# A graph network kernel whose weight products run as fillers: Wg and Wm's parts moved ahead of the third batch, the second bias row moved behind the chunk loop

## The reference

```
A = zeros(1024,1024); A[src,dst] += weight;  deg = sum(A, 1);  dinv = deg > 0 ? deg^-0.5 : 0
h = x
for l in 0, 1:                      # D = diag(dinv)
    h = D A D h
    h = h Wg[l] + bg[l]
    h = leaky_relu(h Wm[l] + bm[l], 0.01)
x = layernorm(x + h)
# second block: edge counts C with self loops, dis = (in-degree)^-0.5
h = relu(C' (x W1) + b1);  h = C' (h W2) + b2       # C' = diag(dis) C^T diag(dis)
x = layernorm(x + h)
```

## Time and profile before

| | |
|---|---|
| median of 3 runs | 334.9 us (334.63 to 335.05) |
| profiled execution | 335.47 us |
| its span | 333.6 us |
| TensorE busy | 314.5 us (94%) |
| VectorE busy | 189.0 us (57%) |
| ScalarE busy | 122.0 us (37%) |
| GpSimd busy | 49.9 us (15%) |

### The profile page before, as it was taken

How to read it: one execution, slowest core, us unless ns; L and a number is a source line. 1 busy time by engine, 2 the same in 40 slices (tenths; PEclk the granted TensorE clock), 3 DMA queues, 4 the chain that set the end, 5 groups by cost and what they waited for, 6 DMA issues and landing times.

```text
span 333.6 us, 4919 instructions
## 1 busy us (share of the span) xinstructions
PE 314.5 (94%) x1977; PEld 259.7 (78%) x1977; DVE 189.0 (57%) x333; ACT 122.0 (37%) x253; POOL 49.9 (15%) x54
## 2 busy tenths in 40 slices
PE   2878999998999999999999999999999999999993
PEld 1767786876788888888888888888888888888882
DVE  6998999714544611165643457675953444225664
ACT  3637889546434401134432013233702444220000
POOL 2100000001005970100000011121680000001111
PEclk9999999999999999999999999999999999999998
DMA  6270000700000000000700000006100000000121
GB/s 211 66 254 2 3 2 0 249 6 2 3 0 1 2 0 0 2 0 0 238 15 0 2 0 0 0 4 226 61 2 0 0 0 2 0 4 33 63 84 73
DMA packets 8590, 13.43 MB, mean 40 GB/s; under 512 B 1906, under 2 KB 2290, under 8 KB 8564
## 3 DMA queue, kind: packets, MB, share of 16 engines
q1 hardware_dynamic: 8564, 13.05, 11.6%
HBM read 10.95 MB, written 2.10 MB: 39 GB/s over the span
## 4 chain that ended last, share of the span: by engine, by line
PE 88%; DVE 7%; issue 2%; ACT 1%; DMA 1%; POOLq 0%; POOL 0%; SPq 0%; ACTq 0%
PE psum L650 75%; PE psum L708 6%; PE psum L636 3%; DVE hot L1004 2%; PE psum L755 1%; DVE sel L996 1%; PE psum L830 1%; DVE hot L999 1%; PE psum L692 1%; DVE wm_low L1089 1%; DVE wgt_low L1076 1%; PE psum L714 1%; DMA src_i<-in_src 1%; PE psum L864 1%; ACT hot L455 0%
## 5 line engine op out<-in xcount | busy, mean ns | idle before, releaser
L441 POOL TENSOR_TENSOR small<-small 128x1 f32<-128x1 f32 x16 | 11.9, 742 | 161.6 <-DVE small L1272 161.6
L708 PE MATMUL psum<-hot,sel 128*128 128x96 bf16 x512 | 32.3, 215 | 2.1 <-DVE hot L1004 1.3
L708 PEld LDWEIGHTS psum<-hot,sel 128*128 128x128 bf16 x512 | 28.4, 101 | 7.5 <-issue 6.9
L650 PE MATMUL psum<-at_high,x_high 128*128 128x512 f32 x64 | 25.8, 403 | 0.6 <-DVE x_low L1200 0.6
L1076 DVE SCALAR_TENSOR_TENSOR y_low<-psum,small,y_high 128x512 fp32r<-128x512 f32 x16 | 11.9, 750 | 24.2 <-ACT y_high L455 24.2
L650 PE MATMUL psum<-at_low,x_high 128*128 128x512 f32 x64 | 25.1, 392 | 0.0
L650 PE MATMUL psum<-y_high,at_high 128*128 128x512 f32 x64 | 25.0, 391 | 0.0
L650 PE MATMUL psum<-cnt,x_high 128*128 128x512 f32 x64 | 25.0, 390 | 0.0
L650 PE MATMUL psum<-at_high,x_low 128*128 128x512 f32 x64 | 25.0, 390 | 0.0
L650 PE MATMUL psum<-cnt,x_low 128*128 128x512 f32 x64 | 25.0, 390 | 0.0
L650 PE MATMUL psum<-y_low,at_high 128*128 128x512 f32 x64 | 24.9, 390 | 0.0
(11 more groups left out here) (185 smaller groups left out, 755.3 us busy)
## 6 DMA issues: line engine op xcount, KB each, us to landing
wg_raw<-in_L_gnn_W_gcn SPq DMA_DIRECT2D x2, 1024.0 KB, 5.5
x_raw<-in_x SPq DMA_DIRECT2D x1, 2048.0 KB, 10.3
xs<-in_x SPq DMA_DIRECT2D x1, 2048.0 KB, 9.3
w_raw<-in_L_gnn_W SPq DMA_DIRECT2D x2, 1024.0 KB, 8.1
out<-xs SPq DMA_DIRECT2D x8, 256.0 KB, 2.0
wm_raw<-in_L_gnn_W_mlp SPq DMA_DIRECT2D x1, 1024.0 KB, 8.2
wm_next<-in_L_gnn_W_mlp SPq DMA_DIRECT2D x1, 1024.0 KB, 8.8
bias_bc<-in_L_gnn_b SPq DMA_DIRECT2D x1, 256.0 KB, 8.2
```

The source lines that it names most:

```text
L441: pool.tensor_tensor(r[:, 1:2], r[:, 0:1], power[:, 0:1], ALU.pow).then_inc(rstd_ready, 1)
L650: ins = pe.matmul(dest, s, m, start=first and n == 0, stop=end and n == len(pairs) - 1, skip_group_check=True)
L708: ins = pe.matmul(sums[1 if k == 0 else 0], stationary, moving, start=False, stop=False, skip_group_check=True)
```

## The change

Wg of layer 0 is transposed ahead of chunk 0 (`FIRST = -1`, behind the clearing of the first two regions), its low parts and Wm's are made between batches 1 and 2 of VectorE's list, and all later fillers move to earlier chunks. Batches 4 and 5 are no longer shared: VectorE makes their fifth part. `bias1` and `biasb1` are made behind the loop, among the adjacency's transposes and products, and get a row tile of their own; their bank is in the ring among the `at` tiles. The load of the row for `biasb1` is issued behind that of x and behind chunk 99's region.

```diff
-    SHARED = {4: {21: 6, 27: 10}, 5: {40: 16}, 7: {66: 8, 73: 8}}
+    SHARED = {7: {66: 8, 73: 8}}
...
+        next_rows = at("next_rows", B2, [3, D], F32)
...
-        fillers = {3: [("wgt0", 0, 0, KD)], 10: [("wgt0", 1, 0, KD), ("wgt0", 2, 0, KD)], 15: [("wgt0", 3, 0, KD)],
-                   27: [("wc0", 0, 0, KD)], 31: [("wc0", 1, 0, KD), ("prep", 4, 0, KD)], 34: [("wc0", 2, 0, 2)],
-                   40: [("wc0", 2, 2, KD), ("wc0", 3, 0, 2)], 47: [("wc0", 3, 2, KD), ("bias0", 0, 0, KD)],
-                   53: [("biasb0", 0, 0, KD), ("wgt1", 0, 0, KD), ("wgt1", 1, 0, KD)],
-                   60: [("wgt1", 2, 0, KD), ("wgt1", 3, 0, KD)], 66: [("bias1", 0, 0, KD)],
-                   73: [("biasb1", 0, 0, KD), ("wc1", 0, 0, 2)], 79: [("wc1", 0, 2, KD)], 86: [("wc1", 1, 0, 2)],
-                   92: [("wc1", 1, 2, KD)], 99: [("wc1", 2, 0, 2)], 105: [("wc1", 2, 2, 3)], 112: [("wc1", 2, 3, KD)],
-                   CH - 1: [("wc1", 3, 0, KD)]}
+        FIRST = -1
+        fillers = {FIRST: [("wgt0", i, 0, KD) for i in range(KD)],
+                   7: [("wc0", 0, 0, KD)], 8: [("wc0", 1, 0, KD)], 15: [("wc0", 2, 0, 2)], 21: [("wc0", 2, 2, KD)],
+                   27: [("wc0", 3, 0, KD)], 31: [("bias0", 0, 0, KD), ("prep", 4, 0, KD)],
+                   34: [("biasb0", 0, 0, KD), ("wgt1", 0, 0, KD), ("wgt1", 1, 0, KD)],
+                   40: [("wgt1", 2, 0, KD), ("wgt1", 3, 0, KD)], 60: [("wc1", 0, 0, KD)], 63: [("wc1", 1, 0, 2)],
+                   73: [("wc1", 1, 2, 3)], 79: [("wc1", 1, 3, KD)], 86: [("wc1", 2, 0, 2)],
+                   92: [("wc1", 2, 2, 3)], 99: [("wc1", 2, 3, KD), ("wc1", 3, 0, 1)], 105: [("wc1", 3, 1, 2)],
+                   CH - 1: [("wc1", 3, 2, KD)]}
...
-        loads = {15: [16], 31: [32], 47: [48, 64], 73: [80], 86: [96], 105: [112]}
+        loads = {15: [16], 27: [32], 31: [48], 60: [64], 63: [80], 86: [96], 99: [112]}
...
         for j in range(NB):
             in_ring("at", j, FILL)
+            if j in (2, 3):
+                in_ring("bias1" if j == 2 else "biasb1", 0, FILL)
...
             sp.wait_ge(done["biasb0"], 1)
-            sp.dma_start(bias_rows[2:3, :], bm[1:2, :]).then_inc(bm_in, 16)
-            sp.wait_ge(done["biasb1"], 1)
             sp.wait_ge(scaled, G * len(SHARED))
             sp.dma_start(x_raw[:], x.rearrange(by_k, p=P)).then_inc(x_in, 16)
+
+            sp.wait_ge(region_done, 1 + closing.index(99))
+            sp.dma_start(next_rows[2:3, :], bm[1:2, :]).then_inc(bm_in, 16)
...
-                if c == 3:
-                    split_wm(0, range(3))
-                if c == closing[0]:
-                    split_wm(0, range(3, KD))
-                if c == 47:
+                if c == FIRST:
+                    split_wm(0, range(KD))
+                if c == 31:
                     split_wm(1, range(KD))
...
             for j in range(NB):
                 upper_x(j)
                 if j + 1 < NB:
                     upper_at("at", 0, j + 1)
+                if j in (1, 2):
+                    upper_fill("bias1" if j == 1 else "biasb1", 0)
...
+            for r in range(2):
+                clear(r)
+            for name, i, k0, k1 in fillers[FIRST]:
+                filler(name, i, k0, k1)
...
             for j in range(3):
                 turn_adjacency("at", 0, j)
+            filler("bias1", 0, 0, KD)
             pe.wait_ge(evacuated, copies(NR - 1))
...
                 if j + 3 < NB:
                     turn_adjacency("at", 0, j + 3)
+                if j == 0:
+                    filler("biasb1", 0, 0, KD)
...
             make_all(1)
+            for i in range(KD):
+                lower_fill("wgt0", i)
+            lower_wm(0)
             make_all(2)
-            make(3, 0)
-            lower_fill("wgt0", 0)
-            for k in range(1, 5):
-                make(3, k)
-            lower_fill("wgt0", 1)
-            lower_fill("wgt0", 2)
-            lower_wm(0)
-            lower_fill("wgt0", 3)
+            lower_fill("wc0", 0)
+            make_all(3)
+            lower_fill("wc0", 1)
             make_all(4)
+            lower_fill("wc0", 2)
             check_windows()
             dve.wait_ge(spill_ready, 1)
             make_hw()
-            lower_fill("wc0", 0)
-            lower_fill("wc0", 1)
+            lower_fill("wc0", 3)
             make_all(5)
+            add_ends(0)
             take_flag()
-            lower_fill("wc0", 2)
-            add_ends(0)
+            lower_wm(1)
+            for i in range(KD):
+                lower_fill("wgt1", i)
             make_all(6)
-            lower_fill("wc0", 3)
-            make(7, 0)
-            lower_wm(1)
-            for i in range(2):
-                lower_fill("wgt1", i)
-            for k in range(1, 5):
-                make(7, k)
-            for i in range(2, KD):
-                lower_fill("wgt1", i)
             add_ends(1)
+            make_all(7)
+            lower_fill("wc1", 0)
             make_all(8)
-            make(9, 0)
-            make(9, 1)
             add_ends(2)
-            for k in range(2, 5):
-                make(9, k)
-            lower_fill("wc1", 0)
+            make_all(9)
             lower_fill("wc1", 1)
```

More of the change, by code:

```diff
@@ L515, in upper_fill @@
                 elif name.startswith("bias"):
-                    if name == "bias1":
-                        act.wait_ge(done["biasb0"], 1)
-                    copy(bias_rows[0:2, :], bank(name)[0:2, :]).then_inc(taken[name], 1)
+                    copy((next_rows if name == "bias1" else bias_rows)[0:2, :], bank(name)[0:2, :])\
+                        .then_inc(taken[name], 1)
                 else:
@@ L747, in filler @@
                     else:
-                        ins = pe.matmul(b, ones3[:], bias_rows[:], start=True, stop=True)
+                        ins = pe.matmul(b, ones3[:], next_rows[:], start=True, stop=True)
                 else:
@@ L771, in _ @@
                 for r in range(NR):
-                    if opening[r] == c:
+                    if r >= 2 and opening[r] == c:
                         clear(r)
```

## The result

The changed kernel takes 347.55 us (median of four runs, 347.23 to 348.48), the kernel before 334.98 in the same runs: ratio 1.0381, interval 1.0359 to 1.0404. Forecast were 341.7 and slower, so the sign and the place held and the size was too small by 5.9. The profiled execution is the 348.48 one (span 346.7), 13.0 above the profiled one of before and 6.3 above the 342.2 of the working.

What follows compares the result with a forecast made beforehand. TensorE's stream sets the end, with VectorE the bound before 26.46 us. 5.3 + 0.4 + 1.05 = 6.75 on the profiled 335.47 gives 342.2, or 341.7 for the median; range 338.4 to 344.6.

Steps and rivals of the forecast that it cites:

- The stop at chunk 34: After chunk 34, TensorE stands at wgt1 1 from 36.9 to 42.35 until VectorE's flag, issued behind batch 5: 5.4 us.
- The second tie: wgt1 3 needs wgt1 0's low part, behind the flag in VectorE's queue, at 45.4: 0.6 us more waiting.
- The uncovered closings: Chunks 47, 53 and 66 have no filler behind them, so TensorE waits for evacuations: 0.88, 0.78 and 0.78 us.
- The wait of batch 5 for the degree matmuls: VectorE cannot start batch 5 until degree matmuls behind chunk 34 have run: it waits from 33.6 to 35.0.
- Behind the loop: After the chunk loop, moved bias1 costs 0.4 us before the first adjacency product, and biasb1 costs 1.05.
- Rival (3): VectorE's queue order does not hold TensorE; stop shorter than 1.5 us, end at 333.8 us; chance 0.06.
- Start, up to 14.8 us: By 14.8 us TensorE has done Wg's transposes and 8 chunks, idled 2.4 us, and begins the product Wg Wm.
- T: Start of TensorE's work behind the last chunk: forecast at 83.7 us, 5.3 later than before (78.38).
- batch 7's scaling: ScalarE's scaling in two blocks of 2.12 us delays evacuations and chunk 80: TensorE waits 1.95 us.
- The slow product: First product at 14.8 us might run at half speed, 5.6 us instead of 2.8: +2.5, not taken.
- Rival (1): Slow restart: TensorE runs at half pace after the stop, wgt1 1 and chunks 35 to 40; 342.5 us; chance 0.27.
- the offsets: Loading chunk offsets is hidden in most places, at worst four times 0.25 us, 0 to +1; taken as 0.

Runs made afterwards that it cites:

- e1: Changed kernel with the flag's steps moved in front of batch 5 in VectorE's list; 344.60 us.
- e3: Kernel before with only the bias part of the change (bias1 and biasb1 behind the loop); 335.00 us.
- e2: Changed kernel with the flag, Wm's low parts and the first two Wg low parts of layer 1 in front of batch 5; 342.02 us.
- e4: Changed kernel with the first 16 chunk offsets loaded behind the clears and Wg's transposes instead of ahead of them; 343.77 us.
- e13: Changed kernel with VectorE's list reordered to fill its waits and the early degree matmuls behind chunk 20 instead of 34; 342.29 us.
- e14: e13 with e4's edit added; 342.25 us.
- e15: e14 with products wc0 0 and 1 behind chunks 14 and 15 and all of wc0 2 behind 21; 343.67 us.
- e7: Kernel before with only the early part: layer 0's Wg and Wm work by the new list, layer 1's fillers where they were; 341.02 us.
- e9: The changed kernel once more, unaltered; 346.75 us (345.94 to 348.91).
- e5: Changed kernel with 22 spare products on TensorE ahead of wgt1 1, in the stop; 344.67 us.
- e6: Changed kernel with ScalarE's share of batches 4 and 5 kept as in the kernel before; 349.61 us.
- e10: Changed kernel with five spare matmuls behind chunk 7, ahead of the first product Wg Wm; 345.26 us.
- e11: Kernel before with only batch 4's fifth part given back to VectorE; 334.79 us.
- e12: e11 plus e3's bias part, against the kernel before; 334.93 us.
- e8: Kernel before with Wm's low parts made by GpSimd instead of VectorE; 338.25 us.

## Why the prediction was right and where it failed

**Right.** The stop at chunk 34: forecast 5.4 from 36.9, ended by the flag, in front of wgt1 1; measured 5.42, the same place and releaser, from 41.0. The second tie as well (e1). The uncovered closings: forecast 0.88, 0.78, 0.78, measured 0.75, 0.65, 0.65. The wait of batch 5 for the degree matmuls: 1.4 forecast, 1.05 measured. Behind the loop: 1.45 forecast, 1.13 measured (0.1 up to the first product, 1.05 for biasb1), and e3 shows both moves by themselves. Rival (3), that VectorE's order would not hold TensorE, is out, with e2 as the nearest to it.

**The step that failed** is "Start, up to 14.8 us", with the pace of the product behind it. The profiled execution, step by step ("late by" is what each adds):

| step | forecast | measured | late by |
|---|---|---|---|
| first product starts | 14.8 | 17.32 | 2.5 |
| first product's pace | 12 matmuls in 2.83 | in 4.42, 9 of them at 0.43 each | 1.6 |
| from there to the stop | 19.3 | 19.3 | 0.0 |
| end of the stop | 42.35 | 46.43 | none of its own |
| wgt1 and the chunks behind the stop | full pace | 0.50 clock | 1.5 |
| around chunk 99 | 0 | 0.77 + 0.22 idle | 1.0 |
| T | 83.7 | 90.26 | sum 6.6 |
| from T to the end | +1.45 | +1.13 | -0.3 |

Sum of what was off: 6.3, the gap between 342.2 and 348.48. In the row on chunk 99 two smaller errors cancel. Counted from start to start, as the forecast did, the two gaps of "issue" are 1.3, and batch 7's scaling cost 1.6 instead of 1.95.

The start was 2.5 late for a reason that I had costed at zero: the clears stood behind the load of 16 offsets, in an engine that till then had had a wait for VectorE to hide it. "Hidden in most places" was true of the places I looked at and false of the one where the wait had been removed (e4: about 2). Behind that the transposes ran at half pace from 9.84 to 13.25, near the upper bound that I had given (3.6), and VectorE waited for each high part. The granted clock reads 1.00 there (10 to 13 us), as it does at the slow transposes of before, so this spell shows in the durations only.

The slow product I had as a bound of +2.5 and chose the fast value "since it kept it over the shorter idle times before". The longest such gap of before was 1.32 (at 17.46), so it had no row for one of 2. The slow product came in the profiled run and not in all: the four fast profiles show that not every execution has it, and there the start had reached full pace sooner. Rival (1) was the right mechanism; I let it end with chunk 40 and priced it at 0.8 net; it reached through wgt1 2 and 3 (eight transposes 1.83 at 49.99, against 1.03 in the earlier trace rows) and cost 1.5 net. The upper ends that the prediction gives for what before does not show (1 for the offsets, 0.8, 2.5, and 0.8 for the restart) add up to 5.1, which is 346.8; the range stopped at 344.6, as if only one of them would come. All four came: the offsets at twice their bound, the start's own lateness at some 0.5, the product at 1.6, the restart at 1.5.

**What the median means.** All eight times of the changed kernel lie from 345.94 to 348.91, and the profiled ones are the slowest of their groups. With the fast first product the forecast's gap is about 4.7, not 6.3, and still more than the range allowed for: the fastest of the eight is above its upper end of 344.6.

**Beneath the single waits** is one cause that the forecast named and didn't follow through: up to 26 us VectorE is the bound. The change puts low parts ahead of its batches, so that it waits for ScalarE and TensorE between (6.2 up to batch 5, before 1.0), and hands it the fifth parts of batches 4 and 5. Batch 5 starts at 39.0, where the forecast had 35.0 and before 31.07. Of the 7.9 to before, 5.2 is more waiting, 0.9 a fifth part, and 1.2 the low parts of two more blocks of the product. Each order of VectorE's queue tried (e1, e2, e13, e14, e15) shows another item of it as the one awaited, and none has a median under 342.

**Open.** The effects overlap, so 5.9 for the early part (e7), 5.5 for the order (e2), 3.8 for the offsets (e4) and 5.3 for the filled waits (e13) don't add up to 12.6. The "issue" gap of 0.7 to 1.05 in the wc1 product of chunk 99 stands beside x's 2 MB load, asked for at 70.5 and landing 10.4 later. Of the profiles with this filler at chunk 99, it is in the six where that load took 10.2 to 10.4 (the changed kernel, e4, e9, e13, e14, e15) and in none of the five where it took 9.1 to 9.4 (e1, e2, e5, e6, e10). Before has two such gaps of 0.39 and 0.24 at 67.14 and 71.32, with a load of 10.3. Whether one causes the other, or a third thing both, no run shows. Why the slow restart comes only in some executions is not settled either. No version tried beats the kernel before; e3, e11 and e12 equal it.

## What to carry to other kernels

Before work is moved into one engine's idle time, look at which engine that idle time waits for: if the move adds to that engine's in-order queue or makes it wait, the bound grows and the idle time reappears later, in front of whatever its queue holds last. Price an idle or light stretch of TensorE twice, once as the wait and once as work at half pace behind it, and add all such terms for the worst case instead of weighing them one by one. When the first wait of a stream is taken away, look at what it was hiding, register loads and descriptor issues among it.

## What the runs showed of the hardware that was not expected

- Loading 16 chunk offsets into registers ahead of TensorE's first clears stood beside 2.4 of "issue" (the changed kernel, 8.16). Moved behind the transposes, it let the clears start 1.8 earlier, and 1.2 of "issue" came ahead of chunk 0 (e4, 12.53).
- The granted clock fell to 0.74 or 0.75 in 15:20 behind a gap of only 2.0 in three of seven profiles of the same stream; in the other four it was 1.00 behind gaps of 2.3 to 2.5. The three had reached full pace later ahead of the gap (chunks 0 to 7 busy 1.96 to 2.07 against 1.66 to 1.73). The Trainium skill ("TensorE: Matmul & The Clock Gate", section "Part 1: The HAM clock gate (the "warmup" mystery)") says that the number of slow matmuls at a kernel's start differs from run to run of one kernel; at this gap, in the middle of one, it is 9 or none.
- In e7 the clock fell to 0.66 in 40:45 with TensorE busy 4.86 of the 5 us, behind 35 matmuls of 24 columns and eight smaller ones and no idle time over 0.54.
- In e5 the clock was 0.69 in 40:45 although TensorE was busy all of it: the slow part follows the lull before 39.7 and the spare work itself bears it.
- Two-input bf16 products of VectorE (128x1536) took 1.93 instead of 0.90 beside two-input subtractions on GpSimd, and the first `hot` 1.42 instead of 0.95 (e8). A 128x512 subtraction of this kind is 1.95 on GpSimd beside these products (four in 7.79 from 12.53) and 0.6 on VectorE.
